# Edge count of a four-layer graph network: the joined weights and the projection move between its windows, x.T comes by chunks, norm's rows use column groups

## The chip, the cores and the metric

The kernel runs on one core of a Trainium2 chip. The metric is the device time of one execution in microseconds (us), lower is better. An engine is named as in the profile: PE or TensorE (matmul; PEld is its weight load), DVE or VectorE, ACT or ScalarE, POOL or GpSimd, SP or SyncE.

## The reference

Four attention layers over one graph of 1250 nodes, 40000 edges sorted by target, and 768 features. The first part is two GAT layers over all edges and self loops, on a normalised x, with a skip projection:

```python
x_norm = layer_norm(x, norm_g, norm_b)
out1 = gat_conv(x_norm, src, dst, W1, a_src1, a_dst1, b1, 4, 192, N)     # layer A
out2 = gat_conv(out1, src, dst, W2, a_src2, a_dst2, b2, 2, 96, N)        # layer B
x1 = _layernorm(x + concat([x, out2]) @ Wu + bu)
h = elu(rgat_conv(x1, W1r, q1, k1, b1r, src, dst, edge_type_3, 4, 192))  # layer C, 3 relations
out = _layernorm(x1 + rgat_conv(h, W2r, q2, k2, b2r, ..., 1, 768))       # layer D

def gat_conv(x, src, dst, W, a_src, a_dst, bias, H, C, n):
    h = (x @ W).reshape(n, H, C)
    e = leaky_relu((h * a_src).sum(-1)[src] + (h * a_dst).sum(-1)[dst], 0.2)
    alpha = softmax of e over the edges of one target
    return segment_sum(alpha[:, :, None] * h[src], dst).reshape(n, H * C) + bias
```

## The kernel before

Attention is done densely. A first stage, the **edge count**, builds the matrix of edge numbers (source by target, one for each relation), and the layers multiply exponentials by it. Targets are cut into 80 **windows** of 16 (`NW`). For a window VectorE and ScalarE make one-hot matrices of 6 chunks of 125 edges: `one_hot_lo` for the source within its tile (4 chunks on ScalarE as |x| and relu, 2 on VectorE, L1907) and `one_hot_hi` for target, relation and source tile (6 on VectorE, L1911). TensorE multiplies them (6 matmuls, L1011) into one of three PSUM banks, and ScalarE saves the bank to `counts` (L1454). The one-hot slots hold three windows: VectorE's window w needs TensorE's window w-3.

Between the windows each engine does other work of layer A, at places written out by hand. `spread(w, (a, b), n)` distributes n units over windows a to b-1; the three engines run the same list, ScalarE one window later.

- **M units** (`M_UNITS` = 15 over `M_WINDOWS` = (1, 25)). Unit 0: `scores_of_b`. Units 1 to 12: `joined`, half of 128 rows of W1 times W2 and the score vectors, copied by ScalarE to `wg`. Unit 13: `norm_rows`, norm_b and norm_g times `wg` as two rows, 12 matmuls with a stationary operand of 2 columns; ScalarE copies them to `rows2` with `scale2` (L1403). Unit 14: `norm_spread`: the mean row (`mean_mm`) and then the constant row (`crow_mm`) are spread over all partitions.
- **x statistics** (`STATS_WINDOWS` = (7, 17)): VectorE, one of ten tiles of x a window (L1824, L1826). After window 20 (`SQRT_AFTER`) ScalarE takes the square root, for which it loads a table (L1414); VectorE's reciprocal of it stands after its window 21 (L1896).
- **x.T**: x.T is loaded into the place of the x tiles, so SyncE waits for all ten statistics (`stats_done`), then issues six loads of 128 rows (L588). The first projection group waits for all six.
- **Centring** (`CENTRE_AFTER` = (28, 31)): VectorE, `wg * g - mean`, six instructions for each half (L1902), after `mean_mm`.
- **G units** (20 over `G_WINDOWS` = (29, 80)): `g_unit(n)`, one tile of x.T times one half of `wg`, 6 matmuls (12 instructions, L995); ScalarE scales and copies it out (L1434). Group 0 comes after window 31, group 19 after window 79.
- **Totals** (`TOTAL_AFTER`): VectorE sums the relations of a finished tile, after windows 33, 35, 37, 39, 45, 53, 61, 69, 77 and the last (L1932 to L1935).

All engines run their program in order; a unit's wait holds all that stands behind it. After group 19 GpSimd loads the weights of layers C and D (L867), and TensorE turns masks (L1071) with score rows between them (L1048). The score rows already use three column groups of the array for matmuls with 32 stationary columns.

Of the kernel before, what the change touches and what calls it, by code (L numbers as in the profile page):

```python
# [20 lines left out]
F32 = mybir.dt.float32  # L21
# [33 lines left out]
ALO = 4  # L55
BANKS = 4
BANKS_USED = 3
M_UNITS = 15
M_WINDOWS, G_WINDOWS, STATS_WINDOWS = (1, 25), (29, 80), (7, 17)
SQRT_AFTER, CENTRE_AFTER = 20, (28, 31)  # L60
TOTAL_AFTER = [max(8 * (t + 1) + 5, 33 + 2 * t) for t in range(T)]


# [93 lines left out]
def gnn_program(nc, t_in, out):  # L157
    with ExitStack() as ctx:
        def sb(name, shape, dt):
            return ctx.enter_context(nc.sbuf_tensor(name, shape, dt))  # L160
# [38 lines left out]
        tab = sb("tab", [1, 192], I32)  # L199
        cols = sb("cols", [P, 114], F32)  # L200
        groups_sel = sb("groups_sel", [96, 8], F32)
        scale2 = sb("scale2", [2, 1], F32)
        sconst = sb("sconst", [P, 4], F32)

        ps = ctx.enter_context(nc.psum_tensor("ps", [P, 8 * 512], F32))
# [1 line left out]
        def bank(b, n=512, at=0):  # L207
            return ps[:, b * 512 + at:b * 512 + at + n]

        def carve(region, at, n, dt=F32):  # L210
            v = region[:, at:at + n]
            return v if dt == F32 else v.bitcast(dt)
# [28 lines left out]
        wt_b = carve(feat, WG1_AT, 2 * D)[0:96, :]  # L241
        rhs = carve(feat, WG_END, 8 * RHS)[0:96, :].rearrange("p (f c) -> p f c", f=8)
        rows2_at = WG_END + 8 * RHS
        rows2 = carve(feat, rows2_at, sum(A_COLS))[0:2, :]
        assert DT * A_COLS[0] <= WG1_AT and WG_END <= 4 * NP and rows2_at + sum(A_COLS) <= T * D

        stage_a = [carve(feat, 4 * NP + i * 2 * HA, 2 * HA) for i in range(3)]
# [325 lines left out]
        def _(sp):  # L573
# [9 lines left out]
            for t in range(T):  # L583
                rn = P if t < T - 1 else LAST
                sp.dma_start(x_tiles[t][0:rn, :], t_in["x"][t * P:t * P + rn, :]).then_inc(x_in[2 * t // T], 16)
            sp.wait_ge(stats_done, T)
            for j in range(DT):
                sp.dma_start(xT[:, j, 0:N], t_in["x_t"][j * P:(j + 1) * P, :]).then_inc(xt_a_in, 16)  # L588


# [243 lines left out]
        @block.gpsimd  # L834
        def _(pool):
            def then(ins):
                pool_n[0] += 1
                ins.then_inc(s_const, 1)
                return pool_n[0]
            pool_n = [0]  # L840
            then(nc.gpsimd.memset(identf[:, :], 0.0))
            then(nc.gpsimd.memset(identb[:, :], 0.0))
            pool.wait_ge(s_const, 2)
            then(nc.gpsimd.affine_select(out=identf[:, :], in_=identf[:, :], compare_op=ALU.not_equal, fill=1.0,
                                         base=0, pattern=[[-1, P]], channel_multiplier=1))
            then(nc.gpsimd.affine_select(out=identb[:, :], in_=identb[:, :], compare_op=ALU.not_equal, fill=1.0,
                                         base=0, pattern=[[-1, P]], channel_multiplier=1))
            then(nc.gpsimd.memset(epsc[:, :], EPS_LN))
            imp = dict(allow_small_or_imprecise_dtypes=True)
            then(nc.gpsimd.iota(iota_lo, [[1, P]], base=0, channel_multiplier=0, **imp))  # L850
            then(nc.gpsimd.iota(iota_hi, [[1, WROW]], base=0, channel_multiplier=0, **imp))
            then(nc.gpsimd.iota(winoff[:, :], [[WKEY, NW]], base=0, channel_multiplier=0, **imp))
            then(nc.gpsimd.iota(iota_w, [[1, NW]], base=0, channel_multiplier=0, **imp))
            then(nc.gpsimd.iota(cid, [[P, 3]], base=0, channel_multiplier=1, **imp))
            then(nc.gpsimd.memset(scale2[:, :], 1.0 / D))
            pool.wait_ge(s_const, 11)
            then(nc.gpsimd.memset(scale2[0:1, :], 1.0))
            assert pool_n[0] == 12
            pool.wait_ge(stats_done, T)
            nc.gpsimd.memset(xT[:, :, N:NP], 0.0).then_inc(xt_a_zero, 1)  # L860


            pool.wait_ge(*sems[A].proj_mm.at(2 * T))
            for i, (c, r, h) in enumerate(WT_HALVES):
                if i >= 3:
                    pool.wait_ge(v_done, i - 2)
                pool.dma_start(wt_half[i], t_in["wt_" + c.name][r].rearrange("(f p) d -> p f d", p=P)  # L867
                               [:, :, h * (D // 2):(h + 1) * (D // 2)]).then_inc(wt_in[i % 3], 16)
            end_phase(pool, 0)
            pool.wait_ge(u_in, 16 * 2)  # L870
            for j in range(DT):
                w_ = wu_half[j // 3][:, j, j % 3 * P:(j % 3 + 1) * P]
                last = nc.gpsimd.tensor_tensor(w_, w_, identf[:, :], ALU.add)
            last.then_inc(u_diag, 1)
            end_phase(pool, 1)
            nc.gpsimd.memset(b2ext[0:K2, :], 1.0)
            nc.gpsimd.memset(wub[0:K2, :, :], 0.0).then_inc(wub_cleared, 1)
            pool.wait_ge(wub_cleared, 1)
            nc.gpsimd.memset(wub[0:1, :, D:D + 1], 1.0).then_inc(wub_zero, 1)
            for k in range(2, 6):  # L880
                end_phase(pool, k)
# [5 lines left out]
        def _(pe):  # L887
# [43 lines left out]
            def norm_rows():  # L931

                pe.wait_ge(m_copied, 2 * DT)
                for p in range(2):
                    for j in range(DT):
                        last = mm(ps[0:2, (5 + p) * 512:(5 + p) * 512 + A_COLS[p]], bgcol[:, j, :], wg[p][:, j, :],
                                  start=(j == 0), stop=(j == DT - 1))
                last.then_inc(rows2_mm, 1)

            def norm_spread():  # L940


                pe.wait_ge(rows2_copied, 2)
                own = lambda i: identf[0:2, i:i + 1].broadcast_to([2, P])
                for p in range(2):
                    last = mm(bank(3 + p, A_COLS[p]), own(1), rows2[:, p * A_COLS[0]:p * A_COLS[0] + A_COLS[p]],
                              start=True, stop=True)
                last.then_inc(mean_mm, 1)
                for f in range(8):
                    mm(bank(7, HA), b1col[:, f:f + 1].broadcast_to([96, P]), rhs[:, f, 0:HA], start=(f == 0), stop=False)  # L950
                for h in range(4):
                    at = h // 2 * A_COLS[0] + h % 2 * HA
                    last = mm(bank(7, HA), own(0), rows2[:, at:at + HA], start=False, stop=(h == 3))
                for q in range(2):
                    at = 2 * HA + q * A.RH
                    last = mm(bank(7, A.RH, 256), own(0), rows2[:, at:at + A.RH], start=(q == 0), stop=(q == 1))
                last.then_inc(crow_mm, 1)

            def m_unit(i):
                if i == 0:  # L960
                    scores_of_b()
                elif i <= 2 * DT:
                    joined(i - 1)
                elif i == 2 * DT + 1:
                    norm_rows()
                else:
                    norm_spread()

            def turn_a_rows():

# [409 lines left out]
        def _(act):  # L1380
# [4 lines left out]
            def m_unit(i):  # L1385
# [7 lines left out]
                elif i <= 2 * DT:  # L1393
                    j, p = (i - 1) // 2, (i - 1) % 2
                    act.wait_ge(m_done, i)
                    o = bank(3 + p, 2 * RHS).rearrange("p (h c) -> p h c", h=2)
                    nc.scalar.activation(wg[p][:, j, 0:2 * HA].rearrange("p (h c) -> p h c", h=2), o[:, :, 0:HA], ACT.Copy)
                    nc.scalar.activation(wg[0][:, j, 2 * HA:].rearrange("p (q h) -> p h q", q=2)[:, 2 * p:2 * p + 2, :],
                                         o[:, :, HA:RHS], ACT.Copy).then_inc(m_copied, 1)
                elif i == 2 * DT + 1:  # L1400
                    act.wait_ge(rows2_mm, 1)
                    for p in range(2):
                        nc.scalar.activation(rows2[:, p * A_COLS[0]:p * A_COLS[0] + A_COLS[p]],  # L1403
                                             ps[0:2, (5 + p) * 512:(5 + p) * 512 + A_COLS[p]], ACT.Copy,
                                             scale=scale2[:, 0:1]).then_inc(rows2_copied, 1)
                else:
                    act.wait_ge(crow_mm, 1)
                    nc.scalar.activation(brow[:, 0:H2W], bank(7, H2W), ACT.Copy)
                    nc.scalar.activation(brow[:, H2W + 1:HA], bank(7, HA - H2W - 1, H2W + 1), ACT.Copy)
                    nc.scalar.activation(sconst[:, :], bank(7, A.RH, 256), ACT.Copy).then_inc(crow_saved, 1)  # L1410
# [22 lines left out]
                        last.then_inc(sa_done, 1)  # L1433
                nc.scalar.activation(stage_a[n % 3], bank(5 + n % 2, 2 * HA), ACT.Copy, scale=rstd).then_inc(s.proj_ev.sem, 1)  # L1434

            act.wait_ge(s_const, 12)
            act.wait_ge(keys_ready, 1)
            act.sem_inc(win_saved, BANKS)
            def one_hot_lo(u, w, free, made, slots):
# [371 lines left out]
        def _(dve):  # L1811
# [25 lines left out]
            v.memset(cmin, 1.0e4)  # L1837
            link(v.memset(cmax, -1.0))
            v.memset(x_tiles[T - 1][LAST // 32 * 32:, :], 0.0).then_inc(s_last, 1)
            dve.wait_ge(s_const, 12)  # L1840
            dve.wait_ge(s_chunkin, 32)
            tail = NCH - 2 * P
            v.tensor_scalar(winc[:, 0:2, :], dstc[:, 0:2, :], W_SHIFT, None, ALU.logical_shift_right)
# [675 lines left out]
```

## Time and profile before

| | us |
|---|---|
| median of 3 runs | 1941.62 |
| lowest, highest | 1939.76, 1941.85 |
| profiled execution | 1941.89 |
| its span in the profile | 1940.1 |

The profile describes one execution, 0.3 us above the median of the runs; 1.8 us of its time lie outside the span. A timeline row gives the start, the length (from the first start to the last end of the instructions merged in it), the engine, line and operation, and in brackets the engine's idle time before it and what ended it.

### The profile page before, as it was taken

How to read it: one execution, taken by the hardware profiler on the slowest of the kernel's cores; microseconds unless marked ns; L12 is line 12 of the kernel's file. 1: busy time of each engine (PE TensorE's matmuls, PEld its weight loads, DVE VectorE, ACT ScalarE, POOL GpSimd, SP SyncE). 2: the span in 40 equal slices, each digit the busy share in tenths (PEclk: the TensorE clock that was granted, in tenths of full speed). 3: DMA queues.
4: the chain of work that ended last, by engine and by line, in shares of the span. 5: the costliest groups of instructions: out<-in, count | busy, mean ns of one | idle time of the engine just before them, and what ended most of it. 6: DMA issues, size and time to landing. Idle time of an engine off the chain costs nothing. (4 is left out here: it accounts for less than half of the span.)

```text
span 1940.1 us, 24254 instructions
## 1 busy us (share of the span) xinstructions
PE 1795.1 (93%) x8426; PEld 1342.6 (69%) x8427; DVE 1549.8 (80%) x2948; ACT 728.1 (38%) x1247; POOL 18.8 (1%) x38
## 2 busy tenths in 40 slices
PE   5789996599999899999999999997999979999997
PEld 3444554399854465555799999997899965555554
DVE  7868876999667654999999999996557547988996
ACT  5857976544214221111344444342311211322331
POOL 0000001000000000000000000000000000000000
PEclk9889998799999899999999999998999989999999
DMA  6200029642171326676421222111266557767764
GB/s 168 80 4 23 31 75 401 239 131 57 46 223 36 130 77 207 223 259 193 138 80 57 84 59 85 58 58 33 84 207 203 165 186 257 239 224 255 249 213 166
DMA packets 168069, 276.66 MB, mean 143 GB/s; under 512 B 11820, under 2 KB 132387, under 8 KB 164487
## 3 DMA queue, kind: packets, MB, share of 16 engines
q1 hardware_dynamic: 114342, 211.25, 33.6%
q10 hardware_dynamic: 50336, 49.66, 7.9%
q0 software_dynamic: 3264, 14.16, 1.9%
q8 instruction: 69, 1.13, 0.2%
q14 instruction: 58, 0.47, 0.1%
HBM read 219.31 MB, written 55.71 MB: 142 GB/s over the span
## 5 line engine op out<-in xcount | busy, mean ns | idle before, releaser
L1359 PE MATMUL ps<-work 128*128 128x384 f32 (+1 forms) x1050 | 342.3, 489 | 11.4 <-DVE work L2387 11.4
L1359 PEld LDWEIGHTS ps<-work 128*128 128x128 f32 x1050 | 200.2, 191 | 153.2 <-issue 14.4
L1286 PE MATMUL ps<-work 128*128 128x384 f32 (+1 forms) x720 | 237.0, 490 | 4.1 <-ACT work L1649 2.6
L1336 PE MATMUL ps<-counts,work 128*128 128x193 f32 x1440 | 239.3, 327 | 0.1
L1336 PEld LDWEIGHTS ps<-counts,work 128*128 128x128 f32 x1440 | 235.9, 190 | 0.4 <-DVE work L2259 0.4
L1743 ACT ACTIVATE work<-work,s 128x1280 f32<-128x1280 f32 x112 | 152.6, 1363 | 210.0 <-DVE work L2253 210.0
L1286 PEld LDWEIGHTS ps<-work 128*128 128x128 f32 x720 | 136.3, 190 | 101.4 <-issue 15.3
L2259 DVE SCALAR_TENSOR_TENSOR work<-work,counts 128x1280 f32<-128x1280 f32 x112 | 166.4, 1485 | 1.4 <-ACT work L1743 1.3
L1336 PE MATMUL ps<-counts 128*128 128x193 f32 x960 | 160.8, 327 | 1.4 <-POOLq L536 1.4
L1336 PEld LDWEIGHTS ps<-counts 128*128 128x128 f32 x960 | 157.4, 190 | 2.0 <-POOLq L536 2.0
L1911 DVE TENSOR_SCALAR work<-work,winoff 125x480 bf16<-125x480 f16 x480 | 157.7, 397 | 0.4 <-issue 0.3
L1781 ACT ACTIVATE work<-work,s 128x256 f32<-128x256 f32 x150 | 68.0, 500 | 224.0 <-DVE work L2360 223.9
L1336 PE MATMUL ps<-work 128*128 128x198 f32 x800 | 136.2, 334 | 15.9 <-DVE work L2259 15.9
L1011 PE MATMUL ps<-work 125*128 125x480 bf16 x480 | 116.4, 393 | 33.7 <-ACT work L1449 16.6
L1336 PEld LDWEIGHTS ps<-work 128*128 128x128 f32 x800 | 135.7, 192 | 16.4 <-issue 16.4
L2253 DVE SCALAR_TENSOR_TENSOR work<-work,sd 128x1280 f32<-128x1280 f32 x76 | 117.4, 1546 | 7.4 <-PE ps L1336 7.4
L1011 PEld LDWEIGHTS ps<-work 125*128 125x128 bf16 x480 | 47.4, 102 | 98.1 <-issue 52.7
L1444 ACT ACTIVATE work<-work 125x128 f16<-125x128 f16 x320 | 102.1, 394 | 11.6 <-issue 9.9
L1195 PE MATMUL ps<-work 128*128 128x192 f32 (+1 forms) x540 | 99.2, 331 | 2.2 <-DVE work L2102 1.5
L1743 ACT ACTIVATE counts<-counts,s 128x1280 f32<-128x1280 f32 x48 | 65.5, 1364 | 80.1 <-DVE counts L2253 79.2
L1195 PEld LDWEIGHTS ps<-work 128*128 128x128 f32 x540 | 90.8, 192 | 3.5 <-issue 2.3
L1719 ACT ACTIVATE work<-ps 128x384 f32<-128x384 f32 x60 | 29.5, 492 | 166.0 <-PE ps L1286 166.0
(278 smaller groups left out, 2445.9 us busy)
## 6 DMA issues: line engine op xcount, KB each, us to landing
work<-hs_d SPq DMA_DIRECT2D x75, 960.0 KB, 5.3
work<-nomask_d SPq DMA_DIRECT2D x70, 320.0 KB, 3.2
work<-pqrow_d SPq DMA_DIRECT2D x12, 1280.0 KB, 6.4
nomask_d<-work SPq DMA_DIRECT2D x40, 320.0 KB, 7.1
hx_d<-work ACTq DMA_DIRECT2D x60, 192.0 KB, 2.6
counts<-hx_d SPq DMA_DIRECT2D x120, 96.0 KB, 1.9
hs_d<-feat ACTq DMA_DIRECT2D x22, 480.0 KB, 3.6
counts<-pqrow_d SPq DMA_DIRECT2D x6, 1280.0 KB, 6.1
```

The costliest lines, as they stand in the source:

```text
L1011: return mm(bank(b, WROW), oh_lo[slot][0:EC, :], oh_hi[slot][0:EC, :], start=start, stop=False, skip_group_check=True)
L1195: last = mm(bank(at, n_), left[:, j, :], right[:, j, 0:n_], start=(start and j == 0), stop=(j == 2), skip_group_check=True)
L1286: last = mm(bank(n % 4 if i else n % 2, cols), xT[:, j, t * P:(t + 1) * P], wv[:, j, :], start=(j == 0), stop=(j == DT - 1))
L1336: last = mm(sums_at(c, t, u), xe_of(c)[i % RING][:, t * P:(t + 1) * P], hx[:, i % RING, 0:1 + c.width], start=(r == 0 and k == 0 and t % T ...
L1359: last = mm(bank(product_bank(g, i), width), a[:, at * P:(at + 1) * P], h[:, block_, 0:width], start=(m == 0), stop=(m == STEPS_D - 1), sk ...
L1444: last = nc.scalar.activation(lo_abs[0:EC, q * P:(q + 1) * P], iota_lo[0:EC, :], ACT.Abs, bias=nlof[0:EC, bass.ds(c0 + q, 1)])
L1719: nc.scalar.activation(stage[n % 3][:, 0:c.piece], bank(b, c.piece), ACT.Copy).then_inc(s.proj_ev.sem, 1)
L1743: nc.scalar.activation(w_, w_, ACT.Exp, bias=s02[:, k, bass.ds(rh, 1)], scale=0.8).then_inc(s.exp_done.sem, 1)
L1781: nc.scalar.activation(w_, w_, ACT.Exp, bias=s02[:, p + q * TH, r:r + 1], scale=0.8).then_inc(d_exp, 1)
L1911: return v.tensor_scalar(oh_hi[slot][0:EC, :], iota_hi[0:EC, :], winoff[0:EC, bass.ds(w, 1)], keyf[0:EC, bass.ds(ch, 1)], ALU.add, ALU.is_ ...
L2253: v.scalar_tensor_tensor(xe_of(c)[i % RING][:, 0:n_], p_, sd[:, k, bass.ds(rh, 1)], q_, ALU.add, ALU.max).then_inc(s.x_ready.sem, 1)
L2259: v.scalar_tensor_tensor(w_, w_, 3.0e38, counts[:, rel, k, lo:lo + n_], ALU.min, ALU.mult).then_inc(s.p_ready.sem, 1)
```

## The change

Four things in the edge count:

- the windows after which units stand: the M units in windows 1 to 17 instead of 1 to 24, the projection groups in 22 to 79 instead of 29 to 79, statistics in 4 to 17, the square root after window 18, the two centrings after 20 and 22. Group 0 comes after window 24; groups are 2.9 windows apart instead of 2.55;
- x.T by chunks: the load of chunk j waits only for the statistics of the x tiles that lie where it goes (2, 4, 5, 7, 9, 10 of them);
- norm's rows: the stationary operand is 32 columns wide, the six row blocks go to three column groups of the array (partitions 0, 32 and 64 of the result), and the rows are summed over the groups when they are spread, by a selecting column of `groups_sel` over 96 partitions;
- their spread is two units, `mean_spread` and `bias_spread`, a window apart.

```diff
-M_UNITS = 15
-M_WINDOWS, G_WINDOWS, STATS_WINDOWS = (1, 25), (29, 80), (7, 17)
-SQRT_AFTER, CENTRE_AFTER = 20, (28, 31)
+M_UNITS = 16
+M_WINDOWS, G_WINDOWS, STATS_WINDOWS = (1, 18), (22, 80), (4, 18)
+SQRT_AFTER, CENTRE_AFTER = 18, (20, 22)
...
-        scale2 = sb("scale2", [2, 1], F32)
+        scale2 = sb("scale2", [96, 1], F32)
...
-        rows2 = carve(feat, rows2_at, sum(A_COLS))[0:2, :]
+        rows2 = carve(feat, rows2_at, sum(A_COLS))[0:96, :]
...
-            sp.wait_ge(stats_done, T)
             for j in range(DT):
+                sp.wait_ge(stats_done, -(-(j + 1) * NP // D))
                 sp.dma_start(xT[:, j, 0:N], t_in["x_t"][j * P:(j + 1) * P, :]).then_inc(xt_a_in, 16)
...
-            then(nc.gpsimd.memset(scale2[0:1, :], 1.0))
+            for g in range(3):
+                then(nc.gpsimd.memset(scale2[32 * g:32 * g + 1, :], 1.0))
...
                 for p in range(2):
                     for j in range(DT):
-                        last = mm(ps[0:2, (5 + p) * 512:(5 + p) * 512 + A_COLS[p]], bgcol[:, j, :], wg[p][:, j, :],
-                                  start=(j == 0), stop=(j == DT - 1))
+                        g = 32 * (j % 3)
+                        last = mm(ps[g:g + 32, (5 + p) * 512:(5 + p) * 512 + A_COLS[p]], cols[:, 2 * j:2 * j + 32], wg[p][:, j, :],
+                                  start=(j < 3), stop=(j >= 3), tile_position=(0, g), skip_group_check=True)
...
-            def norm_spread():
+            def own_row(i):
+                return groups_sel[:, i:i + 1].broadcast_to([96, P])
+            def mean_spread():
                 pe.wait_ge(rows2_copied, 2)
-                own = lambda i: identf[0:2, i:i + 1].broadcast_to([2, P])
                 for p in range(2):
-                    last = mm(bank(3 + p, A_COLS[p]), own(1), rows2[:, p * A_COLS[0]:p * A_COLS[0] + A_COLS[p]],
+                    last = mm(bank(3 + p, A_COLS[p]), own_row(1), rows2[:, p * A_COLS[0]:p * A_COLS[0] + A_COLS[p]],
                               start=True, stop=True)
                 last.then_inc(mean_mm, 1)
+            def bias_spread():
                 for f in range(8):
                     mm(bank(7, HA), b1col[:, f:f + 1].broadcast_to([96, P]), rhs[:, f, 0:HA], start=(f == 0), stop=False)
...
-                elif i == 2 * DT + 1:
-                    norm_rows()
                 else:
-                    norm_spread()
+                    (norm_rows, mean_spread, bias_spread)[i - 2 * DT - 1]()
```

## Rows read from the trace of the kernel before

**Rows 1.** The page, part 1: busy us (share of the span) xinstructions.

```profile
PE 1795.1 (93%) x8426; PEld 1342.6 (69%) x8427; DVE 1549.8 (80%) x2948; ACT 728.1 (38%) x1247; POOL 18.8 (1%) x38
```

**Rows 2.** Stretches of the edge count: busy us (xinstructions), PEclk, DMA share, GB/s.

```profile
20.00:99.00 79.00, 60.64 (x271) 37.70 (x272) 67.20 (x229) 65.50 (x178) 0.25 (x1) 0.87 0.30 100
99.00:112.00 13.00, 11.40 (x37) 3.11 (x34) 7.39 (x27) 7.21 (x20) 0.00 (x0) 1.00 0.01 2
112.00:126.00 14.00, 14.00 (x42) 10.54 (x42) 2.13 (x8) 2.47 (x10) 0.00 (x0) 0.51 0.00 0
126.00:173.00 47.00, 37.82 (x135) 17.93 (x134) 43.52 (x133) 36.53 (x94) 0.00 (x0) 0.93 0.04 14
173.00:286.00 113.00, 112.47 (x435) 59.40 (x433) 96.92 (x323) 97.65 (x250) 0.22 (x1) 1.00 0.12 42
```

**Rows 3.** Timeline of PE, the first joined unit.

```profile
36.82 2.99 PE L927 MATMUL ps<-feat,counts 96*128 96x199 f32 x8 [0.70 <-ACT feat L1391]
```

**Rows 4.** Timeline of DVE, windows 16 to 27 (start, us, instructions, [idle]).

```profile
73.80 0.42 DVE L1907 TENSOR_SCALAR work<-work 125x128 bf16<-125x128 f16 x2 [0.57 <-issue]
...
77.83 0.42 DVE L1907 TENSOR_SCALAR work<-work 125x128 bf16<-125x128 f16 x2 [0.56 <-issue]
...
80.05 0.41 DVE L1907 TENSOR_SCALAR work<-work 125x128 bf16<-125x128 f16 x2
...
92.16 0.22 DVE L1896 RECIPROCAL sdev<-sdev 128x10 f32<-128x10 f32 x1 [3.17 <-ACT sdev L1414]
...
123.87 0.42 DVE L1907 TENSOR_SCALAR work<-work 125x128 bf16<-125x128 f16 x2 [12.53 <-PE ps L1011]
...
126.09 3.34 DVE L1902 SCALAR_TENSOR_TENSOR feat<-feat,cols,ps 128x402 f32<-128x402 f32 x6
```

**Rows 5.** Timeline of PE, norm's rows, their spread and group 0.

```profile
99.36 8.19 PE L936 MATMUL ps<-feat,cols 128*2 128x402 f32 x24
...
110.47 1.60 PE L946 MATMUL ps<-feat,identf 2*128 2x402 f32 x4 [1.60 <-ACT feat L1403]
112.00 5.62 PE L950 MATMUL ps<-feat,cols 96*128 96x197 f32 x16
...
121.13 7.26 PE L1011 MATMUL ps<-work 125*128 125x480 bf16 x24
...
137.43 4.22 PE L995 MATMUL ps<-feat,work 128*128 128x402 f32 x12
```

**Rows 6.** Timeline of ACT: square root's table load, then starts of three windows.

```profile
90.53 1.28 ACT L1414 ACT_TABLE_LOAD   x1
...
248.32 1.28 ACT L1444 ACTIVATE work<-work 125x128 f16<-125x128 f16 x4 [0.22 <-issue]
...
250.94 1.28 ACT L1444 ACTIVATE work<-work 125x128 f16<-125x128 f16 x4 [0.22 <-issue]
...
253.71 1.27 ACT L1444 ACTIVATE work<-work 125x128 f16<-125x128 f16 x4
```

**Rows 7.** Timeline of DVE, one tile of totals and the next window.

```profile
165.14 0.82 DVE L1932 TENSOR_TENSOR counts<-counts 128x1280 uint16<-128x1280 uint16 x1
...
167.88 0.42 DVE L1907 TENSOR_SCALAR work<-work 125x128 bf16<-125x128 f16 x2 [0.81 <-DVE counts L1935]
```

**Rows 8.** Timeline of PE, a projection group and two windows.

```profile
181.46 4.22 PE L995 MATMUL ps<-feat,work 128*128 128x402 f32 x12
185.52 2.61 PE L1011 MATMUL ps<-work 125*128 125x480 bf16 x12
```

**Rows 9.** Timeline of PE, group 19, and score rows of the next stage.

```profile
281.33 4.14 PE L995 MATMUL ps<-feat,work 128*128 128x394 f32 x12
...
308.10 1.49 PE L1048 MATMUL ps<-work,cols 128*32 128x384 f32 x12
```

**Rows 10.** Timeline of POOL, the first weight loads of the next stage.

```profile
285.78 2.86 POOL L867 DMA_DIRECT2D work<-in_wt_c  x3 [208.20 <-PE ps L995]
```

**Rows 11.** Timeline of SP's queue, the loads of x.T.

```profile
77.30 3.15 SPq L588 DMA_DIRECT2D work<-in_x_t  x6
```

More of the change, by code:

```diff
@@ L856, in _ @@
             pool.wait_ge(s_const, 11)
-            then(nc.gpsimd.memset(scale2[0:1, :], 1.0))
-            assert pool_n[0] == 12
+            for g in range(3):
+                then(nc.gpsimd.memset(scale2[32 * g:32 * g + 1, :], 1.0))
+            assert pool_n[0] == 14
             pool.wait_ge(stats_done, T)
@@ L952, in norm_spread @@
                     at = h // 2 * A_COLS[0] + h % 2 * HA
-                    last = mm(bank(7, HA), own(0), rows2[:, at:at + HA], start=False, stop=(h == 3))
+                    last = mm(bank(7, HA), own_row(0), rows2[:, at:at + HA], start=False, stop=(h == 3))
                 for q in range(2):
                     at = 2 * HA + q * A.RH
-                    last = mm(bank(7, A.RH, 256), own(0), rows2[:, at:at + A.RH], start=(q == 0), stop=(q == 1))
+                    last = mm(bank(7, A.RH, 256), own_row(0), rows2[:, at:at + A.RH], start=(q == 0), stop=(q == 1))
                 last.then_inc(crow_mm, 1)
@@ L1403, in m_unit @@
                         nc.scalar.activation(rows2[:, p * A_COLS[0]:p * A_COLS[0] + A_COLS[p]],
-                                             ps[0:2, (5 + p) * 512:(5 + p) * 512 + A_COLS[p]], ACT.Copy,
+                                             ps[0:96, (5 + p) * 512:(5 + p) * 512 + A_COLS[p]], ACT.Copy,
                                              scale=scale2[:, 0:1]).then_inc(rows2_copied, 1)
-                else:
+                elif i == 2 * DT + 3:
                     act.wait_ge(crow_mm, 1)
@@ L1434, in g_unit @@
                 nc.scalar.activation(stage_a[n % 3], bank(5 + n % 2, 2 * HA), ACT.Copy, scale=rstd).then_inc(s.proj_ev.sem, 1)
-            act.wait_ge(s_const, 12)
+            act.wait_ge(s_const, 14)
             act.wait_ge(keys_ready, 1)
@@ L1839, in _ @@
             v.memset(x_tiles[T - 1][LAST // 32 * 32:, :], 0.0).then_inc(s_last, 1)
-            dve.wait_ge(s_const, 12)
+            dve.wait_ge(s_const, 14)
             dve.wait_ge(s_chunkin, 32)
```

## The prediction

> **What bounds the kernel now.** I read the page first: TensorE is busy 93% of the span and VectorE 80% [rows 1]. That is an average, and the change touches only the first stage, the edge count, so I cut that stage into stretches [rows 2]. The reader should see three regimes. Up to 99 us no engine is full, TensorE 61 of 79. From 99 to 126 TensorE is full while VectorE and ScalarE do almost nothing (2.1 and 2.5 of 14 us from 112 on), and from 112 its clock is half. From 173 to 286 TensorE is full, at full clock (112.5 of 113 us), and the others wait for it.
>
> The stage ends with projection group 19, started at 281.33 [rows 9] and, 4.14 later, done at 285.5. The next stage hangs on it alone: GpSimd, idle for 208.2 us, issues its weight loads at 285.78 when that group's matmuls are done [rows 10], and TensorE itself goes on to the mask transposes behind it. No other step of the change reaches later, so every microsecond by which group 19 ends earlier is one off the total.
>
> Groups start only after window 31, at 137.4 us [rows 5]; by then TensorE has idled and afterwards it has a backlog. The timelines of the stretch show why groups can't start earlier: VectorE loses 3.17 us to ScalarE's square root, and 12.53 us behind the spread of norm's rows [rows 4], which runs as one block on TensorE from 110.47 to 121.13 [rows 5].
>
> **The change, part by part.** Prices per window first. VectorE: 80.05 - 77.83 = 2.22 us; with one tile of x statistics 77.83 - 73.80 = 4.03, so a tile is 1.81 [rows 4]; a tile of totals is 167.88 - 165.14 = 2.74 [rows 7]; one centring is 3.34 [rows 4]. ScalarE: 2.62 plain, 2.77 with a group's copy [rows 6]; in the first ten groups there is one small copy more, I take 0.3. TensorE: a group 185.52 - 181.46 = 4.06, a window (2.61 - 0.16)/2 = 1.22 [rows 8].
>
> Windows 0 to 17. The twelve joined units go from windows 4 to 21 into windows 3 to 14, one a window. TensorE has room: a joined unit is 2.99 us for 8 instructions even at half clock [rows 3], about 1.4 at full, with 1.2 for the window. The first one now stands behind window 3 and still can't begin before ScalarE's copies, at 36.8 [rows 3]; window 4 falls behind it and ends near 41 (2.99 and 1.2 later), and VectorE, which now counts a tile in windows 5 and 6, wants it some 2 us earlier. The old order has stalls of about that length between its windows 7 and 9, so I count no difference; without that cover it costs 2. All ten x tiles are counted by window 17, not 16, and VectorE's work up to there is the same, so it ends at about 80.5 (before: 80.05 for window 17 [rows 4]).
>
> x.T by chunks: six loads, issued in 3.15 us at 77.3, all behind the tenth statistic [rows 11]. Now four of them go during the statistics and the last at about 80.5. The first group needs them at about 109, so both the old and the new order are hidden. SyncE's queue has nothing behind them until the first group's output. Worth 0; without that cover the last chunk would cost its landing, a few us. Two more GpSimd memsets for the scale lie under VectorE's wait for the first edges: 0.
>
> Norm's rows: 24 instructions, 8.19 us [rows 5]. In column groups of three they have the form of the score rows, 12 instructions of 384 columns in 1.49 us [rows 9]. For 24 of about 400: 2 x 1.49 x 1.04 = 3.1 us, a gain of 5.1 on TensorE; bounds 2.7 (8.19/3, the three groups side by side) and 8.2 (no overlap at all). The Trainium skill's page "TensorE: Matmul & The Clock Gate", section "Measured speedup vs the span model", gives 2.38 times for three column tiles; by it the unit would be 3.4 us, an estimate, and the sum 0.3 longer at most. ScalarE's two copies go from 2 to 96 partitions with the same columns: 0, as its time goes by columns.
>
> The spread: mean (1.60) and bias (9.13, all of it at half clock, so 4.6 at full) [rows 2, 5] are parted by a window. What was 12.53 us of VectorE idle is split. But the bias unit now stands ahead of window 18, and ScalarE's square root waits for the save of window 18, and VectorE's window 20 waits for the square root. So: window 17 ends on TensorE at 80.1, bias 84.8, window 18 at 86.0; the save of 0.6 and, from the start of the table load to VectorE's reciprocals, 92.16 - 90.53 = 1.63 [rows 4, 6] make 88.3, and VectorE is back at 89.1. It had been done with window 19 at 84.9, so the old stall of 3.17 becomes 3.4. Then VectorE does windows 20 to 24 and both centrings: 5 x 2.22 + 6.6 = 17.7, so 106.8. Window 24 on TensorE adds 1.4, and 1.2 more since after such waits it mostly runs at half clock: group 0 starts at 109.4 instead of 137.4.
>
> Windows 25 to 79 with 20 groups, one per 2.9 windows instead of 2.55. TensorE needs 1.22 + 4.06/2.9 = 2.62 per window, ScalarE 2.67 to 2.73, VectorE 2.22 + 2.74/8 = 2.56. Before, TensorE needed 1.22 + 4.06/2.55 = 2.81 and set the pace alone. Now ScalarE does, by a hair: 47 windows x 2.70 = 126.9. Windows 33 to 40 hold four totals and are VectorE's: 8 x 2.22 + 4 x 2.74 = 28.7. The row copies of ScalarE for A's scores add 1.4. Three engines within 0.15 us of each other lose something to each other; no row shows that balance, its bounds are 0 and 0.3 a window (VectorE's totals not hidden at all, below), and I take 0.05, since three windows are buffered: 2.6. Sum 159.6; window 79 ends at 269.0, group 19 at 273.1.
>
> So the stage ends at 273.1 instead of 285.5: 12.4 us off. The profiled execution took 1941.9 for its span of 1940.1; minus 12.4 is 1929.5, and the median of the runs is 0.3 below the profiled one: 1929.
>
> **The rivals.** (a) The bias unit runs at half clock again. For it: rows 2 show 14 us of dense matmuls at half clock, bias among them, without a rise. Against: it fell there after norm's spread of 2 rows, which now are 96, and an idle 1.6 us. Price 9.13 - 4.6 for bias and 1.2 for the next window, 5.8 rounded up: 1935. The Trainium skill's page "TensorE: Matmul & The Clock Gate", Part 1, says that the low clock is the default and that activity releases it. By that rule bias, dense as it is, would run at 2.4 GHz and the total would be the forecast's; rows 2 at 0.51 for 14 us of full TensorE disagree.
>
> (b) The balance costs nothing and the windows buffered hide most of VectorE's four totals: 2.6 + 4 off, 1923. For it: VectorE gains 0.5 us a window on ScalarE outside those windows; against it: it can lead by three windows only.
>
> (c) The totals of windows 45 to 77 and 85 are exposed, as nobody waits for TensorE any more: five of 2.74 are 13.7, half of it 6.9: 1936, all of it: 1943, no change. For it: before, VectorE's waits for TensorE swallowed them; against it: 20.5 us per 8 windows are below ScalarE's 21.6.
>
> (d) Slower. TensorE stays at half clock through the joined units, now one per window: 2 x (1.22 + 1.4) = 5.24 for each of windows 3 to 14, 62.9 us against VectorE's 12 x 2.22 + 7 x 1.81 = 39.3. That is 23.6 more: 1952. It decides from 12.4 + 3.9 = 16.3 us on, some nine of those twelve windows. For it: clock 0.87 over 20 to 99 and an idle of 3.5 us ahead of the first unit; against it: a TensorE so full has risen again within a few us elsewhere there.
>
> **Numbers.** Forecast 0.52, (a) 0.22, (b) 0.08, (c) 0.12, of which 0.04 still shows as faster, (d) 0.06. Faster by over 0.2% (3.9 us, about what a measurement of this kernel can tell from no change) 0.86; within 0.08; slower 0.06. The range reaches to (b) and past (a) and half of (c): 1923 to 1938.
>
> **What would show it.** Norm's rows near 3.1 us; group 0 near 109; VectorE's wait for the square root 3 to 4 us (9 if (a)); TensorE no longer full from 173 on but with small waits for ScalarE and VectorE in it; group 19 ending near 273; the mask stage and all behind it unchanged in length. I am wrong if group 0 starts early and group 19 still ends near 285, if norm's rows take 8 us, or if a later stage changes its length.

## The result and the profile after

| | us |
|---|---|
| before, median of 4 runs beside it | 1940.69 (1939.43 to 1941.85) |
| after, median of 4 runs | 1925.18 (1923.37 to 1927.75) |
| ratio, 95% interval | 0.9916, 0.9904 to 0.9929 |
| span of the profiled execution, before and after | 1940.1 and 1923.3 |

The change makes the kernel faster by 0.84%, some 16 us; forecast were 12.6 below the median shown, in a range of 1923 to 1938. TensorE's share hardly moves, 92% of a shorter span (the page, part 1 of after, beside [rows 1]):

```profile
PE 1777.4 (92%) x8426; PEld 1334.4 (69%) x8427; DVE 1549.1 (81%) x2948; ACT 727.3 (38%) x1247; POOL 19.1 (1%) x40
```

Stretches of the edge count after, as in [rows 2]:

```profile
20.00:99.00 79.00, 60.78 (x310) 39.81 (x310) 62.72 (x207) 61.93 (x172) 0.25 (x1) 0.90 0.32 104
99.00:112.00 13.00, 8.07 (x24) 3.07 (x25) 13.00 (x42) 7.20 (x19) 0.00 (x0) 0.66 0.01 2
112.00:126.00 14.00, 14.00 (x55) 7.38 (x54) 12.33 (x45) 11.71 (x31) 0.00 (x0) 1.00 0.04 15
126.00:173.00 47.00, 43.22 (x162) 21.92 (x160) 42.66 (x137) 41.12 (x109) 0.00 (x0) 0.96 0.07 27
173.00:270.00 97.00, 94.58 (x368) 49.03 (x366) 85.74 (x288) 86.02 (x219) 0.00 (x0) 1.00 0.12 40
```

See the third row. From 112 to 126 TensorE was full at half clock, with VectorE busy for 2.1 us [rows 2]; now it is full at full clock, and VectorE and ScalarE work beside it. The timeline of TensorE after answers to [rows 3, 5, 9]:

```profile
36.36 2.99 PE L929 MATMUL ps<-feat,counts 96*128 96x199 f32 x8 [3.57 <-ACT feat L1398]
...
75.13 2.88 PE L940 MATMUL ps<-feat,cols 128*32 128x402 f32 x24 [1.26 <-ACT feat L1405]
77.94 1.39 PE L1018 MATMUL ps<-work 125*128 125x480 bf16 x6
80.94 1.61 PE L952 MATMUL ps<-feat,groups_sel 96*128 96x402 f32 x4 [1.61 <-ACT feat L1410]
82.39 1.38 PE L1018 MATMUL ps<-work 125*128 125x480 bf16 x6
83.60 2.83 PE L959 MATMUL ps<-feat,cols 96*128 96x197 f32 x16
...
112.11 4.22 PE L1002 MATMUL ps<-feat,work 128*128 128x402 f32 x12
...
265.62 4.14 PE L1002 MATMUL ps<-feat,work 128*128 128x394 f32 x12
```

Norm's rows take 2.88 us (8.19 before), group 0 starts at 112.11 (137.43), and group 19 ends at 265.62 + 4.14 = 269.8 (285.5). The stage is 15.7 us shorter. GpSimd's weight loads follow at once, at 270.07. VectorE after, against [rows 4]: its 12.53 us behind the spread are gone, while its wait for the square root has grown from 3.17 to 5.66 us:

```profile
41.91 0.42 DVE L1914 TENSOR_SCALAR work<-work 125x128 bf16<-125x128 f16 x2 [3.80 <-PE ps L1018]
...
91.96 0.21 DVE L1903 RECIPROCAL sdev<-sdev 128x10 f32<-128x10 f32 x1 [5.66 <-ACT sdev L1421]
```

The first matmul of layer A's attention starts at 370.52 after and 384.89 before, 14.4 earlier; the span ends 16.8 earlier. So the mask stage gives back 1.3 of the 15.7 and the stages behind it gain 2.4. Both lie within what traces differ by there: from the end of group 19 to that matmul it is 99.4 us before and 98.5 to 102.2 in the thirteen other traces, and a second trace of the kernel after has its matmul at 370.34 but ends at 1929.9, not 1923.3.

### The profile page after: what moved, and what is told of

It is laid out like the page before. It is cut to its first block and busy times, and to the rows that moved or that the text cites. A ratio compares the mean times of both kernels' runs of the same rounds, so it can differ in the third digit from the quotient of the medians.

```text
span 1923.3 us, 24256 instructions
## 1 busy us (share of the span) xinstructions
PE 1777.4 (92%) x8426; PEld 1334.4 (69%) x8427; DVE 1549.1 (81%) x2948; ACT 727.3 (38%) x1247; POOL 19.1 (1%) x40
## 5 line engine op out<-in xcount | busy, mean ns | idle before, releaser
L1343 PEld LDWEIGHTS ps<-work 128*128 128x128 f32 x800 | 135.6, 192 | 15.8 <-issue 15.7
L1018 PE MATMUL ps<-work 125*128 125x480 bf16 x480 | 113.0, 384 | 30.0 <-DVE work L1918 17.8
L1018 PEld LDWEIGHTS ps<-work 125*128 125x128 bf16 x480 | 46.9, 101 | 91.8 <-issue 44.0
L1750 ACT ACTIVATE counts<-counts,s 128x1280 f32<-128x1280 f32 x48 | 65.5, 1364 | 80.1 <-DVE counts L2260 79.2
```

Source lines behind the costliest of these rows:

```text
L1018: return mm(bank(b, WROW), oh_lo[slot][0:EC, :], oh_hi[slot][0:EC, :], start=start, stop=False, skip_group_check=True)
L1343: last = mm(sums_at(c, t, u), xe_of(c)[i % RING][:, t * P:(t + 1) * P], hx[:, i % RING, 0:1 + c.width], start=(r == 0 and k == 0 and t % T ...
L1750: nc.scalar.activation(w_, w_, ACT.Exp, bias=s02[:, k, bass.ds(rh, 1)], scale=0.8).then_inc(s.exp_done.sem, 1)
```

## The experiments

Two theories stood against each other at first. **P**: the places do it, since projection group 0 starts 25 us earlier and the stage's end follows it. **G**: the column groups do it, by taking time from TensorE ahead of a stretch in which TensorE is full. A third was formed from the traces of the first four experiments. **S**: in the new places TensorE's units stand ahead of ScalarE's square root, for which VectorE waits, so that what is in front of it counts. Theory B, in the expectation of experiment 6, is P's opposite: a late start is worked off.

Each ratio is to runs of the kernel before on the same chip: one chip for experiments 1 to 4 (before 1941.66), one for 5 to 8 (1942.85), one for 9 to 12 (1943.1). Single executions lie up to some 7 us off the median of their kernel, and a trace shows one execution: that of experiment 3 took 1941.24, 6.4 above its median, that of 4 took 1928.10, 3.1 below. What follows group 19 takes between 1655 and 1661 us in the fourteen traces, the time of the execution less the stage's end. So an effect of a few microseconds is read at the stage's end, with the total beside it.

**1. The places alone.** The kernel before with the new windows; norm's rows, the one-unit spread and x.T's wait as they were.

```diff
-M_WINDOWS, G_WINDOWS, STATS_WINDOWS = (1, 25), (29, 80), (7, 17)
-SQRT_AFTER, CENTRE_AFTER = 20, (28, 31)
+M_WINDOWS, G_WINDOWS, STATS_WINDOWS = (1, 17), (22, 80), (4, 18)
+SQRT_AFTER, CENTRE_AFTER = 18, (20, 22)
```

> The kernel before with only the windows of the change: joined units in windows 3 to 14, norm's rows after 15, the whole spread after 16, statistics, square root, centrings and groups as in the changed kernel. x.T waits for all statistics, norm's rows are 12 matmuls with 2 columns one after another, the spread is one unit from 2 rows. Theory P (places): the gain is the earlier start of group 0 and the wider spacing of the groups; TensorE's units are a detail. Then this takes most of it, 12 to 13 of the 15.5 us: about 1928. Theory G (TensorE's time): before, TensorE is full from the first group to the last, and what the change gives is the TensorE time removed ahead of it, norm's rows 8.2 to 2.9 us and the spread's stretch at half clock (about 14 us of the stage, worth 7). Then it all stays in this kernel, only earlier: 1936 to 1941, with norm's rows and spread taking some 20 us between windows 15 and 18 and VectorE idle behind them.

Measured: 1937.97, ratio 0.9978 (0.9964 to 0.9991). Group 0 starts at 121.96, 15.5 earlier than before, and group 19 ends at 275.49 + 4.14 = 279.6, only 5.9 earlier. That is against P; the time lies in G's forecast. The wait for the square root is 15.0 us, from which S was formed:

```profile
101.88 0.21 DVE L1896 RECIPROCAL sdev<-sdev 128x10 f32<-128x10 f32 x1 [14.99 <-ACT sdev L1414]
```

**2. The column groups alone.** The kernel before with norm's rows in three column groups and spread from 96 partitions, in one unit, at the old places.

```diff
...
-                        last = mm(ps[0:2, (5 + p) * 512:(5 + p) * 512 + A_COLS[p]], bgcol[:, j, :], wg[p][:, j, :],
...
+                        last = mm(ps[g:g + 32, (5 + p) * 512:(5 + p) * 512 + A_COLS[p]], cols[:, 2 * j:2 * j + 32], wg[p][:, j, :],
...
```

> The kernel before with only norm's rows in three column groups and their spread from 96 partitions, as one unit, at the old places. Theory P: TensorE saves 8.2 - 2.9 = 5.3 us ahead of its full stretch, and group 0 still comes after window 31: about 1935. Theory G: the clock does not fall either, as the 2-row matmul that stood before the fall now has 96 rows; 5.3 and about 7 for the half clock are saved ahead of a stretch in which TensorE is full: 1928 to 1930. If the clock falls all the same, both give 1935; the clock of the stretch behind the spread tells which.

Measured: 1931.89, 0.9949 (0.9931 to 0.9968), between the two forecasts and nearer to G's. Group 19 ends at 272.10 + 4.14 = 276.2, 9.3 earlier. Norm's rows give 5.1 of it (3.11 us for 8.19). The spread behind them gives the next part (the timeline of TensorE in this kernel):

```profile
99.31 3.11 PE L938 MATMUL ps<-feat,cols 128*32 128x402 f32 x24
...
105.36 1.77 PE L948 MATMUL ps<-feat,groups_sel 96*128 96x402 f32 x4 [1.62 <-ACT feat L1405]
106.93 4.38 PE L952 MATMUL ps<-feat,cols 96*128 96x197 f32 x16
111.15 1.50 PE L955 MATMUL ps<-feat,groups_sel 96*128 96x197 f32 x8
```

The rows of bias, L952, take 4.38 us where they took 5.62 [rows 5], and L955 1.50 where L953 took 2.99: here the clock has come back within the unit. VectorE waits 8.18 us behind it instead of 12.53.

**3. The change without column groups.** All else of the change, with norm's rows of 2 columns.

```diff
...
-                        last = mm(ps[g:g + 32, (5 + p) * 512:(5 + p) * 512 + A_COLS[p]], cols[:, 2 * j:2 * j + 32], wg[p][:, j, :],
...
+                        last = mm(ps[0:2, (5 + p) * 512:(5 + p) * 512 + A_COLS[p]], bgcol[:, j, :], wg[p][:, j, :],
...
```

> The changed kernel with norm's rows again as 12 matmuls with 2 columns and the spread from 2 rows; all else as changed, the two spread units apart. Theory P: 5.3 us more on TensorE, all of it ahead of the square root on which VectorE waits: 1930. Theory G: the half clock comes back as well with the 2-row matmuls, in the bias unit or the window before it, 5 to 7 us more: 1933 to 1937.

Measured: 1934.87, 0.9967 (0.9954 to 0.9979), as G has it. Norm's rows 8.19 again, the square root's wait 14.9, group 0 at 123.06, group 19 done at 281.4. The column groups are thus worth 11.6 us at the stage's end in this pair of traces, and some 10 us by the ratios of the totals (0.9967 against 0.9916), for 5.3 us of matmul. More came with them. Behind norm's rows of 2 columns the clock is at half here, and at full where they are in column groups (stretches of this kernel, then of the kernel after):

```profile
86.00:94.00 8.00, 7.83 (x21) 4.96 (x22) 1.03 (x4) 4.39 (x12) 0.00 (x0) 0.57 0.00 0
...
78.00:86.00 8.00, 6.39 (x32) 4.29 (x32) 7.41 (x27) 5.39 (x14) 0.25 (x1) 1.00 0.48 161
86.00:92.00 6.00, 4.56 (x27) 3.04 (x25) 0.34 (x2) 2.99 (x8) 0.00 (x0) 1.00 0.00 1
```

**4. One unit for the spread.** The change with mean and bias together after window 16.

```diff
-M_UNITS = 16
-M_WINDOWS, G_WINDOWS, STATS_WINDOWS = (1, 18), (22, 80), (4, 18)
+M_UNITS = 15
+M_WINDOWS, G_WINDOWS, STATS_WINDOWS = (1, 17), (22, 80), (4, 18)
...
-                    (norm_rows, mean_spread, bias_spread)[i - 2 * DT - 1]()
+                    (norm_rows, lambda: (mean_spread(), bias_spread()))[i - 2 * DT - 1]()
...
```

> The changed kernel with mean and bias again one unit, after window 16 (15 units in windows 2 to 16). Both theories: bias moves one window earlier, so window 18 and the square root come earlier by up to one window, but window 17 comes later by the bias unit's 4.8 us. Theory P sees a gain in the parting: 1927 to 1928. Theory G sees TensorE's work unchanged: 1925, no difference beyond 1.5 us either way.

Measured: 1931.22, 0.9946 (0.993 to 0.9963), slower than either forecast. Square root's wait 6.7, group 0 at 114.14, group 19 done at 272.0, 2.3 later than in the change. The ratios put the totals farther apart, 0.9946 against 0.9916: how much parting the units is worth is known only as some 2 to 6 us.

**5. The square root a window earlier.**

```diff
-SQRT_AFTER, CENTRE_AFTER = 18, (20, 22)
+SQRT_AFTER, CENTRE_AFTER = 17, (20, 22)
```

> The changed kernel with ScalarE's square root after window 17 instead of 18 and VectorE's reciprocal after its window 18 instead of 19. Nothing of TensorE's work moves. Theory S (the square root): what a unit on TensorE costs ahead of window 18 costs it because ScalarE's square root waits for that window's save and VectorE for the square root; the wait is 5.7 us in the changed kernel and 15.0 where norm's rows are the old ones. Then the square root comes at 84.3 instead of 90.3, VectorE waits 2 us instead of 5.7, and all behind it is earlier by 3 to 4: 1921 to 1922. Theory G (TensorE's time): TensorE's instructions and their lengths are the same, so 1925 within a microsecond.

Measured: 1924.69, 0.9913 (0.9897 to 0.9928). The wait falls to 1.9, group 0 starts at 108.40, and group 19 ends at 266.5, 3.3 earlier than in the change: the stage follows S. The total does not: it was forecast at 1921 to 1922 by S and 1925 by G, and does not separate from the change's.

**6. Groups from window 29 again.** The change, with its projection groups as late as before.

```diff
-M_WINDOWS, G_WINDOWS, STATS_WINDOWS = (1, 18), (22, 80), (4, 18)
+M_WINDOWS, G_WINDOWS, STATS_WINDOWS = (1, 18), (29, 80), (4, 18)
```

> The changed kernel with the groups' windows as before (29 to 79, group 0 after window 31, one per 2.55 windows). Theory P (places): group 0 starts seven windows later, near 128 instead of 112, the gain of the wider spacing is gone, TensorE is full from there on and ends some 6 to 10 us later: 1931 to 1935. Theory B (balance): windows 25 to 31 alone go at ScalarE's 2.62 us, so group 0 starts near 128, and from there TensorE needs 48 x 1.22 + 20 x 4.02 + 1.1 = 140 us, which ends at 268 to 272, where the changed kernel ends too: 1924 to 1928, the groups' places being worth nearly nothing.

Measured: 1928.59, 0.9927 (0.9914 to 0.994), just above B's 1924 to 1928. The run that decides on P:

```profile
128.39 4.22 PE L1002 MATMUL ps<-feat,work 128*128 128x402 f32 x12
...
268.09 4.14 PE L1002 MATMUL ps<-feat,work 128*128 128x394 f32 x12
```

Group 0 starts 16.3 us later than in the change, group 19 ends 2.5 us later. TensorE has no gap from 173 to 265 (92.00 of 92) as it works off what is late. Against run 8 on the same chip the median is 3.1 higher. P has fallen as the main cause: 16.3 us of start are worth some 3.

**7. Three places mended.** The first joined unit a window later, the square root after 17, the bias unit after 22.

```diff
-SQRT_AFTER, CENTRE_AFTER = 18, (20, 22)
+SQRT_AFTER, CENTRE_AFTER = 17, (20, 22)
+M_AT = [2, *range(4, 16), 16, 17, 22]
...
-                    for i in spread(w, M_WINDOWS, M_UNITS):
+                    for i in (i for i, at in enumerate(M_AT) if at == w):
...
-                    for i in spread(w - 1, M_WINDOWS, M_UNITS):
+                    for i in (i for i, at in enumerate(M_AT) if at == w - 1):
```

> The changed kernel with the square root after window 17, the joined units in windows 4 to 15 (a window later), norm's rows after 16, mean after 17 and the bias unit after window 22, where TensorE waits for VectorE's second centring anyway. Theory S: VectorE sets the pace up to group 0. It gains 3.7 at the square root and, of its 3.8 us of waiting behind the first joined unit, some 2.8, so group 0 starts near 105 to 106 instead of 112 and the total is 1918 to 1920. Theory G: TensorE's time is unchanged, 1925. If the balanced stretch behind it gives back what is gained, the total stays near 1922.

Measured: 1918.83, 0.9879 (0.986 to 0.9897). Group 0 at 103.97, group 19 done at 261.6, TensorE's idle time ahead of the first joined unit 0.53 us instead of 3.57.

**8. x.T in one wait.** The change, with all six loads behind the tenth statistic.

```diff
+            sp.wait_ge(stats_done, T)
             for j in range(DT):
-                sp.wait_ge(stats_done, -(-(j + 1) * NP // D))
```

> The changed kernel with x.T's six loads again behind all ten statistics, so issued from about 81 us on. Both theories: hidden, they land near 95 and group 0 starts at 112: 1925, no difference. A rival is that loads beside the statistics slow VectorE or that the late loads reach group 0's start: 1 to 3 us either way.

Measured: 1925.49, 0.9906 (0.9891 to 0.9921). Group 0 at 112.44, group 19 done at 270.1, both within 0.4 us of the change. The chunks are worth nothing that shows here.

**9 to 11. Once more, on one chip.** The change, the kernel of 5 and the kernel of 7, unaltered.

> The changed kernel once more, on the same chip as the three below, so that they can be set against it and not only against the kernel before. 0.991 to 0.992 of before, as the first time; group 0 near 112 and group 19 near 269.8.

> The kernel with the square root after window 17 again. Its trace showed VectorE's wait fall from 5.7 to 1.9 us, group 0 start 3.7 and group 19 end 3.3 us earlier, but its runs lay with the changed kernel's. Theory S: the 3.3 us are real and the scatter of five runs hid them: ratio 0.990, 3 us below change_again. Theory G: the total doesn't follow: the same ratio as change_again within 0.0007.

> The best kernel again, beside the changed one. Its first run had group 19 end at 261.6 where the changed kernel has 269.8 and a ratio of 0.9879 to before. Expected 6 to 8 us below change_again, 0.987 to 0.988 of before.

Measured: the change 1927.86, 0.9917 (0.9898 to 0.9937); the earlier square root 1926.76, 0.9914 (0.9896 to 0.9932); the mended places 1919.48, 0.988 (0.9861 to 0.9899). Group 19 ends at 270.3, 266.5 and 263.6. The mended places are 8.4 us below the change, the slowest of their six executions (1922.24) below the fastest of its six (1923.19). The earlier square root shortens the stage by 3.8 us in this pair of traces too, but its median is only 1.1 lower with overlapping intervals: its worth in the total stays inconclusive.

**12. The bias unit alone.** The change with that unit after window 22, the square root still after 18.

```diff
+M_AT = [*range(2, 17), 22]
...
-                    for i in spread(w, M_WINDOWS, M_UNITS):
+                    for i in (i for i, at in enumerate(M_AT) if at == w):
...
-                    for i in spread(w - 1, M_WINDOWS, M_UNITS):
+                    for i in (i for i, at in enumerate(M_AT) if at == w - 1):
```

> The changed kernel with only the bias unit moved, from after window 17 to after window 22; square root after window 18 and joined units from window 3 as changed. Theory S: it was the bias unit ahead of window 18 that made ScalarE's square root late, so VectorE's wait for it falls from 5.7 to about 2.4 us, the bias unit fits into TensorE's wait for the second centring, and group 0 starts 3.3 us earlier, near 108.8; about 3 us below change_again. Rival: VectorE's wait is ScalarE's own lag, and stays above 4 us.

Measured: 1922.18, 0.9901 (0.9879 to 0.9924). The median is 5.7 below the change on this chip, where about 3 was forecast, but the intervals overlap and the ratios differ by 0.0016 only, 3 us. The stage shows it surely: the wait for the square root is 2.2 us, group 0 starts at 107.50 and group 19 ends at 265.1, 5.1 earlier. It was the bias unit ahead of window 18 that held the square root.

**All of them on one sheet.** The stage issues the same matmuls in every kernel: 914 to 918 records from 20 us to the end of group 19. So its length is TensorE's busy time and its idle time. The sum row of three stretches (20 to 99, 99 to 126, 126 to the end of group 19) gives both, idle being the length less PE. Of before:

```profile
sum 265.47, PE 236.33 PEld 128.68 DVE 216.63 ACT 208.86 POOL 0.25; mean PE 78.78 PEld 42.89 DVE 72.21 ACT 69.62 POOL 0.08
```

Of after:

```profile
sum 249.76, PE 220.65 PEld 121.21 DVE 216.21 ACT 207.77 POOL 0.25; mean PE 73.55 PEld 40.40 DVE 72.07 ACT 69.26 POOL 0.08
```

Of the mended places:

```profile
sum 241.63, PE 219.95 PEld 118.86 DVE 216.29 ACT 207.64 POOL 0.26; mean PE 73.32 PEld 39.62 DVE 72.10 ACT 69.21 POOL 0.09
```

The last column is the part of the busy time that the low clock cost: the stage cut into stretches of 1 us, and busy time by (1 - PEclk) summed over them. Stretches of 2 us give the same within 0.3 us.

| kernel | stage ends | TensorE busy | TensorE idle | of busy, lost to the clock |
|---|---|---|---|---|
| before | 285.5 | 236.3 | 29.1 | 19.1 |
| 1 places only | 279.6 | 229.6 | 30.0 | 13.0 |
| 2 column groups only | 276.2 | 227.0 | 29.3 | 14.6 |
| 3 no column groups | 281.4 | 233.5 | 27.9 | 15.2 |
| after | 269.8 | 220.7 | 29.1 | 9.6 |
| 9 after, again | 270.3 | 221.4 | 28.8 | 9.9 |
| 4 one unit | 272.0 | 221.0 | 31.0 | 9.7 |
| 6 groups from 29 | 272.2 | 222.7 | 29.6 | 10.0 |
| 8 x.T in one wait | 270.1 | 221.0 | 29.1 | 9.7 |
| 5, 10 square root 17 | 266.5, 266.5 | 220.7, 221.5 | 25.8, 25.0 | 8.5, 8.9 |
| 12 bias after 22 | 265.1 | 220.7 | 24.4 | 8.5 |
| 7, 11 mended | 261.6, 263.6 | 220.0, 219.2 | 21.7, 24.5 | 6.5, 6.8 |

What follows is the plainest result of the study. The change takes 15.7 us from TensorE's busy time and nothing from its idle time. Of the 15.7, norm's rows are 5.3 and the granted clock is 9.5 (19.1 less 9.6). The last 0.9 are small; a window's six matmuls take 1.38 us alone and three windows in one go 3.81, so a denser order also shows less busy time. Before, the clock cost 3.0 us up to 52 us, 6.0 from 52 to 99, 6.8 from 112 to 126 and 3.2 later; after, 3.4 up to 52, none from there to 94, 4.5 from 94 to 112, behind VectorE's wait for the square root, and 1.7 later. The new places alone took 6.7 of busy time, 6.1 of it clock; the column groups alone 9.4, of which 5.1 are norm's rows and 4.5 clock. That is 16.1 together, so the two add up. The totals say so within their scatter too (0.22% and 0.51% against 0.84%). Only the runs 5, 7 and 12 lower the idle time, by 3 to 7 us, and they do it where S says.

## Why the prediction was right, and where it was not

**The end of the stage.** Forecast 273.1, measured 269.8. The direction, the place and the range were right. Group 0 came 2.7 us later than forecast, through two terms mis-sized, and from there the stage was 6.1 shorter, through a third. That these errors stand against each other is luck; the end is off by 3.3 only.

**Norm's rows**: forecast 3.1, bounds 2.7 and 8.2, measured 2.88, and 3.11 in run 2. The Trainium skill's page "TensorE: Matmul & The Clock Gate", section "Measured speedup vs the span model", would have given 3.4; these rows are 8.19 / 2.88 = 2.84 times as fast, where it has 2.38. The measurement decides.

**Windows 0 to 17** was the first term mis-sized. "I count no difference" for the first joined unit, with 2 us if that cover were gone: it was gone. VectorE loses 3.80 and 0.87 us behind it, where its old stalls there were 2.4 together, and is done with window 19 at 86.3, not 84.9. Run 7 puts the unit a window later, and TensorE's idle time there is 0.53.

**The bias unit and the square root** was mis-sized by more. The bias unit took 4.4 us from 83.60 to 87.97, at full clock as forecast (4.6). But I had TensorE's window 17 done at 80.1, and it was done at 83.6. Some 1.4 of that is VectorE's lateness from the first joined unit. The rest, some 2, is the mean unit: it stands ahead of window 17 and itself waits 1.61 us for ScalarE's copies of norm's rows, which the sum did not follow. The copies of bias, 0.4 us, also go ahead of the table load. So VectorE is back at 91.96, not 89.1, its wait 5.66, not 3.4, and group 0 starts at 112.1, not 109.4: 2.7 too early in the forecast. Runs 5 and 12 take that wait away by its two ends.

**Windows 25 to 79** was too long: 159.6, against 265.62 - 112.11 = 153.5. Its part for windows 33 to 40 was exact. The four totals are VectorE's own pace (after):

```profile
132.06 0.82 DVE L1939 TENSOR_TENSOR counts<-counts 128x1280 uint16<-128x1280 uint16 x1
...
139.22 0.81 DVE L1939 TENSOR_TENSOR counts<-counts 128x1280 uint16<-128x1280 uint16 x1
...
146.39 0.82 DVE L1939 TENSOR_TENSOR counts<-counts 128x1280 uint16<-128x1280 uint16 x1
...
153.55 0.82 DVE L1939 TENSOR_TENSOR counts<-counts 128x1280 uint16<-128x1280 uint16 x1
```

They are 7.16 apart, which makes 28.7 for four pairs of windows, the forecast's figure. The other 47 windows took 153.5 - 28.7 = 124.8, or 2.66 each, where the sum had 126.9 + 1.4 + 2.6 = 130.9. The loss of 2.6 by the balance did not come, nor the 1.4 of row copies, and the pace lies between TensorE's 2.62 and ScalarE's 2.70. What TensorE waited for from 112 to 272 is little (the view of waits: us in total, times, longest):

```profile
PE ps L1018 <- DVE work L1918: 4.2, 4, 2.4
PE ps L1018 <- issue: 0.9, 2, 0.7
PE ps L1018 <- ACT counts L1461: 0.7, 1, 0.7
```

So "now ScalarE does, by a hair" was wrong: apart from windows 33 to 40 TensorE sets the pace still (94.58 of 97 us from 173 on). The prediction's first paragraph also called TensorE full from 99 to 126 before; from 99 to 112 it was busy for 11.40 of 13 us, and VectorE for 7.39 [rows 2].

**The reason given** was the weaker part. The prediction cut VectorE's stalls and an earlier group 0, and reached nearly the right figure. The sheet shows that TensorE's idle time did not shrink at all and that run 6, with group 0 at 128.4, loses 2.5 us of the 15.7. The prediction priced norm's rows (5.1) and the half clock of bias (9.13 to 4.6) as steps on the way to group 0, but did not see that norm's rows and the clock, TensorE's own time, would be the whole gain, 5.3 and 9.5. Nor had it a term for the clock from 52 to 99. VectorE's stalls matter as far as they idle TensorE, and over the whole stage they idled it as long as before.

**The rivals.** (a), bias at half clock again, did not come after; it came in part in the kernel's second trace (3.30 us instead of 2.83, square root's wait 7.3) and for all the bias rows in run 1 (5.54). By the Trainium skill's "TensorE: Matmul & The Clock Gate", Part 1, activity releases the low clock: this case's bias after agrees with it, the 14 us at 0.51 of [rows 2] still do not. (b): of its two parts the balance came for nothing, and the total lies near its 1923; its other part, four totals hidden, did not come. (c), exposed totals later on, did not come. (d), slower by a half clock in the joined units, did not come: the clock from 20 to 99 is 0.90, before 0.87. x.T by chunks was worth 0, as forecast (run 8); the GpSimd memsets show nowhere.

**Left open**: what brings the half clock on and how long it stays, for which the last section has the rows, and how much of each single trace's clock would come again: the kernel before was traced once, while the pairs of after, 5 and 7 agree within 0.4 us of clock.

## What to carry to other kernels

Where a stage issues the same instructions on its fullest engine before and after, split its length into that engine's busy and idle time: the sheet says in one line whether a reordering won idle time or busy time. Then look at the granted clock in short stretches, as a mean over a long one hides where it fell. An earlier start of the first unit is worth little where the fullest engine can work off the delay later (16.3 us of start gave 2.5 here); what counts is what that engine does between. A unit moved ahead of another engine's wait must be followed with its own wait included, here the mean unit's 1.61 us for the copies; moving the bias unit by five windows ended the stage 5.1 us earlier.

## What the runs showed of the hardware

- The granted clock after norm's spread differs between kernels with the same matmuls in it. Before: 0.51 over 14 us of full TensorE [rows 2], the bias rows 5.62 us. Places only: they took 5.54, and the clock was back while TensorE was full (stretches of that kernel; PEclk is the third figure from the end):

```profile
88.00:94.00 6.00, 6.00 (x18) 5.36 (x18) 0.00 (x0) 0.00 (x0) 0.00 (x0) 0.53 0.69 279
94.00:100.00 6.00, 5.43 (x30) 3.27 (x29) 0.00 (x0) 2.93 (x10) 0.00 (x0) 1.00 0.00 0
```

  Column groups only: 4.38. After: 2.83 and, in a second trace, 3.30.
- Runs 2 and 3 vary norm's rows and their spread by themselves, and the clock goes with them. In the three kernels with 2 columns (before, 1, 3) it is low for 8 to 14 us soon behind those rows. In the eleven traces with column groups there are 5 us or less: 106 to 111 in run 2, 81 to 85 in the second trace of after, 74 to 79 in run 11, where norm's rows took 4.57 us, and none in the eight others until VectorE's wait for the square root. No run tells apart whether the 2 columns, their 8.19 us or the spread from 2 rows bring it on.
- From 52 to 100 us the low clock cost 6.0 us before and 6.4 in run 2, both with the old places. In all twelve traces with the joined units one a window it cost nothing between 44 and 74.
- The change from 32-column matmuls in column groups back to 128-column ones costs nothing that the trace shows: L940 starts at 75.13, takes 2.88, and the window's L1018 follows at 77.94.
- A switch of ScalarE's table is 1.28 us (L1421 at 90.33 after), but VectorE's wait for the square root behind it was 1.9 to 15.0 us, by what stood ahead of it.
